# Products of key features and values in tiles of 64 columns instead of 32, in an attention and feed-forward layer

## What is computed

```python
q = heads(query, Wq, bq, Sq)            # 16 heads of 32
k = heads(key, Wk, bk, Sk)
v = heads(value, Wv, bv, Sk)
q_prime = relu(einsum('bhnd,fd->bhnf', q, Wqf))     # 64 features per head
k_prime = relu(einsum('bhnd,fd->bhnf', k, Wkf)) * mask
kv = einsum('bhnf,bhne->bhfe', k_prime, v)          # 64 x 32 per head
qkv = einsum('bhmf,bhfe->bhme', q_prime, kv)
k_sum = sum(k_prime, axis=2)
qk_sum = einsum('bhmf,bhf->bhm', q_prime, k_sum)
out = (qkv / (qk_sum + 1e-8)) @ Wo.T + bo
```

## Time and profile before

| | us |
|---|---|
| median of 3 runs | 432.66 (428.31 to 433.16) |
| the profiled execution, its own time | 431.65 |
| its span, first to last instruction | 429.6 |
| mean granted TensorE clock, share of full speed | 0.995 |
| TensorE busy (MATMUL) | 411.4 |
| weight loads busy | 284.4 |
| VectorE busy | 342.3 |
| ScalarE busy | 286.5 |
| GpSimd busy | 145.8 |

### The profile page before, as it was taken

One profiled execution on the slowest core, in us unless ns is written; L12 is line 12 of the kernel. 1 busy time (PEld: TensorE's weight loads), 2 busy tenths in 40 slices (PEclk: granted clock), 3 DMA queues, 4 the chain that ended last, 5 costly groups with the idle time before them and its releaser, 6 DMA issues.

```text
span 429.6 us, 11266 instructions
## 1 busy us (share of the span) xinstructions
PE 411.4 (96%) x4804; PEld 284.4 (66%) x4835; DVE 342.3 (80%) x505; ACT 286.5 (67%) x406; POOL 145.8 (34%) x290
## 2 busy tenths in 40 slices
PE   8989999999999999999989999999999999999995
PEld 4879899988878945844754575575567566464443
DVE  4644659658679959899986897999998798998982
ACT  5655989892155287778449747765873878939960
POOL 0000000003054722483371545547325523344660
PEclk9989999999999999999999999999999999999999
DMA  7992474632050300113323033031213021413065
GB/s 235 418 403 74 169 278 159 287 120 82 24 198 5 108 19 2 32 31 87 73 38 63 0 88 76 11 75 50 51 41 70 14 50 27 84 62 75 1 146 124
DMA packets 51170, 42.42 MB, mean 99 GB/s; under 512 B 43056, under 2 KB 44080, under 8 KB 49200
## 3 DMA queue, kind: packets, MB, share of 16 engines
q1 hardware_dynamic: 51120, 41.70, 32.9%
HBM read 27.01 MB, written 4.19 MB: 73 GB/s over the span
## 4 chain that ended last, share of the span: by engine, by line
PE 52%; DVE 21%; issue 7%; ACT 7%; POOL 6%; DMA 6%; SPq 0%; DVEq 0%; ACTq 0%
PE ps L538 11%; PE ps L407 11%; PE ps L358 6%; PE ps L360 5%; PE ps L359 5%; PE ps L555 4%; DVE zb L974 3%; PE ps L429 2%; PE ps L514 2%; DMA xqT<-xqb 2%; PE ps L448 2%; DVE rows_of L922 2%; DVE tk L985 2%; DVE qol L933 1%; DVE rows_of L917 1%
## 5 line engine op out<-in xcount | busy, mean ns | idle before, releaser
L538 PE MATMUL ps<-tg,xqT 128*128 128x512 bf16 x243 | 58.1, 380 | 4.6 <-DMA xqT<-xqb 2.9
L538 PE MATMUL ps<-tu,xqT 128*128 128x512 bf16 x245 | 59.1, 379 | 1.3 <-issue 0.6
L555 PE MATMUL ps<-td,yqT 128*128 128x512 bf16 x202 | 45.9, 379 | 1.1 <-DMA yqT<-yqb 0.7
L538 PEld LDWEIGHTS ps<-tg,xqT 128*128 128x128 bf16 x256 | 23.5, 98 | 33.1 <-DMA xqT<-xqb 4.0
L538 PEld LDWEIGHTS ps<-tu,xqT 128*128 128x128 bf16 x256 | 24.2, 98 | 31.2 <-issue 3.0
L721 ACT ACTIVATE rb<-zb 128x1024 f32<-128x1024 f32 x29 | 30.6, 1055 | 20.7 <-DVE zb L974 20.5
L974 DVE TENSOR_TENSOR zb<-ps,rb 128x1024 f32<-128x1024 f32 x29 | 35.3, 1218 | 8.2 <-ACT rb L717 8.0
L358 PE MATMUL ps<-aph,wqh 128*128 128x256 f32 x128 | 37.2, 290 | 0.0
L360 PE MATMUL ps<-aph,wkl 128*128 128x256 f32 x124 | 35.4, 286 | 1.8 <-issue 1.8
L985 DVE TENSOR_REDUCE tk<-zb 128x1 f32<-128x1024 f32 x30 | 36.2, 1207 | 1.0 <-POOL zb L1189 0.7
L358 PE MATMUL ps<-aph,wkh 128*128 128x256 f32 x124 | 36.2, 292 | 0.6 <-issue 0.6
(11 more groups left out here) (153 smaller groups left out, 1037.1 us busy)
## 6 DMA issues: line engine op xcount, KB each, us to landing
xs<-in_wg_dram SPq DMA_DIRECT2D x4, 1024.0 KB, 13.9
xs<-in_wu_dram SPq DMA_DIRECT2D x4, 1024.0 KB, 6.6
xs<-in_wd_dram SPq DMA_DIRECT2D x4, 1024.0 KB, 7.9
xs<-in_x_dram SPq DMA_DIRECT2D x8, 512.0 KB, 4.9
out_dram<-xs SPq DMA_DIRECT2D x15, 256.0 KB, 2.0
craw<-in_ctx_dram SPq DMA_DIRECT2D x7, 512.0 KB, 5.8
xs<-in_wk_dram SPq DMA_DIRECT2D x4, 256.0 KB, 5.0
xs<-in_wv_dram SPq DMA_DIRECT2D x4, 256.0 KB, 6.6
```

What stands on the lines that cost most here:

```text
L538: k = pe.matmul(ps[:, b0 + n, :], xqT[:, i % 3, kc, :], tern[w][:, o:o + 512], start=kc == 0, stop=kc == KC - 1)
L555: k = pe.matmul(ps[:, D_BANK[i], :], yqT(i)[:, j, :], tern[2][:, 512 * j:512 * j + 512], start=j == 0, stop=j == 15)
```

## The change

In `key_values`, the inner loop runs over the two heads of a pair instead of over four pieces of 32 features. Each matmul takes all 64 features of a head as its stationary operand, and the two matmuls of a pair lie side by side as two tiles of 128 rows by 64 columns. There are 32 matmuls for a sequence instead of 64, and 256 instead of 512 in all. The results lie in the same places of the same bank.

```diff
@@ -439,13 +439,12 @@
                 for half in range(2):
                     for pr in range(4 * half, 4 * half + 4):
                         for t in range(2):
-                            for c in range(4):
-                                i = 2 * b + t
-                                h = head(pr, c // 2)
-                                o = 256 * (h % 4) + 64 * (h // 4) + 32 * (c % 2)
-                                out = ps[32 * c:32 * c + 32, KV_BANK[b] + half, 33 * (pr % 4):33 * (pr % 4) + 33]
-                                left, right = kp[:, t, o:o + 32], vt[:, i % 4, h // 2, 34 * (h % 2):34 * (h % 2) + 33]
-                                k = pe.matmul(out, left, right, start=t == 0, stop=t == 1, tile_position=(0, 32 * c))
+                            for hd in range(2):
+                                i, h = 2 * b + t, head(pr, hd)
+                                o = 256 * (h % 4) + 64 * (h // 4)
+                                out = ps[64 * hd:64 * hd + 64, KV_BANK[b] + half, 33 * (pr % 4):33 * (pr % 4) + 33]
+                                left, right = kp[:, t, o:o + 64], vt[:, i % 4, h // 2, 34 * (h % 2):34 * (h % 2) + 33]
+                                k = pe.matmul(out, left, right, start=t == 0, stop=t == 1, tile_position=(0, 64 * hd))
                     k.then_inc(*key_values_done.now(b, half))
```

## The result

| | before | after |
|---|---|---|
| median of 20 runs each | 431.61 us (427.83 to 433.16) | 434.83 us (432.36 to 436.19) |
| ratio after to before | | 1.0082, 95% interval 1.0064 to 1.0100 |
| profiled execution, its span | 429.6 us | 430.5 us |

The changed kernel is slower by 0.8%, some 3.5 us by the ratio and 3.2 by the medians. In two later comparisons it was 1.0100 (1.0061 to 1.0140) and 1.0103 (1.0065 to 1.0142) times before. The forecast was 436.5 us, +1.1%. It was made for a profiled execution; that one took 432.49 us, and the two later profiled ones of the same kernel 437.35 and 432.86.

The account below looks back on a forecast made before the run. TensorE, busy 96% of the span, was taken as the bound: profiled 431.65 us plus 4.8 for seven longer blocks plus 0.1 for the eighth gave 436.5 us, range 431 to 441.

Parts of the forecast that it names:

- The load sets the turn: In a tile of 64 columns, the weight load, not the 33-column stream, sets each pass at 57 ns; chance 0.79.
- Block +0.69 us: Each changed block: last start at 1.82 us (0.11 first turn plus 30 turns of 57 ns) against 1.13 before.
- the 86 ns: Longest turn considered, from line 429's whole blocks: 1.37 us for 16 turns; would add 1.6 us a block.
- Seven blocks on the path: TensorE alone bounds the first seven blocks, so each adds its full 0.69 us: +4.8 us.
- The eighth hidden: Behind the eighth block TensorE waits 0.8 us for xqT, so only 0.1 us counted, between nothing and 0.33.
- "Issue" waits left at nothing: Two TensorE waits for no other engine, 0.8 us in all, might go or move; counted zero, kept for the range.
- All inputs come through TensorE, so the rest is rigid: Later stages were taken as a rigid chain, so delay in the blocks would not be swallowed there.
- Both rules of the Trainium skill: MATMUL starts never closer than about 25 ns; loads overlap a MATMUL only across row groups. The prediction set rows against both.
- Handed out: Rival: instruction hand-out, 8.9 ns a pass, paces the block; 0.56 us less each, total about 427.5 us; chance 0.07.
- One after the other: Rival: load and stream cannot overlap within a tile; turn 82 ns, +1.41 us a block, total 442.1 us; chance 0.08.
- No change: Rival: something else is late where the blocks end, so the time stays at 431.65 us; chance 0.06.

Follow-up runs that it names:

- e2: The changed kernel, its two tiles each loading only the first 32 of a head's 64 columns (half the products left out): 428.62 us, ratio 0.9956.
- e3: The changed kernel, tiles of 64 columns, each matmul streaming 1 column instead of 33: 441.08 us, ratio 1.0253.
- e4: The kernel before, four tiles of 32 columns, each matmul streaming 1 column instead of 33: 430.21 us, ratio 1.0010.
- e7: The kernel before with tiles of 64 columns in the first seven blocks and 32 in the eighth: 432.85 us, ratio 1.0054.
- e11: The kernel before, its eighth block alone with 32 matmuls loading 32 columns each (half that block's products left out): 428.42 us, ratio 0.9947.
- e12: The kernel before with tiles of 64 columns in the seventh block alone: 430.24 us, ratio 0.9976 to before.
- e5: The changed kernel again, unchanged, for a second profile: 436.09 us.
- e10: The changed kernel again, unchanged, for a third profile and more runs: 435.83 us.
- e1: The kernel before once more, unchanged, for a second profile: 431.16 us, ratio 1.0008.
- e8: The kernel before with tiles of 64 columns in the eighth block alone, run a second time: 428.56 us, ratio 0.9948.
- e9: The kernel before with tiles of 64 columns in the sixth and eighth blocks: 431.30 us, ratio 1.0024.

## Why the prediction was right

By its own steps:

- *The load sets the turn.* Right, and shown from both sides: a load of 32 columns on the same two tiles gives 1.01 us (e2), a stream of one column changes nothing (e3). The forecast turn was 57 ns, the measured one 58.5 (1.84 us less the first turn of 0.08, over 30). The time for a load of 32 columns was not right: 27 ns was worked out from 128 columns, and e2 and e4 show turns of 32 to 34. The forecast did not use it.
- *Block +0.69 us.* Measured +0.71 from first start to last, +0.73 to the follower. Two small parts were off and cancelled, which is luck: the first turn is 0.08 us, while 0.11 was line 429's (0.03 too long once), and the turn is 58.5 and not 57 (0.045 too short over 30). On the long side, the 86 ns were divided by 16 where 16 passes have 15 intervals; it is 91 ns, and changes nothing in the forecast. The records are longer than forecast, a MATMUL's 223 ns and not 200, a load's 138 and not 130.
- *Seven blocks on the path.* Right: the value products behind a block begin 0.73 later each time.
- *The eighth hidden.* Right. 0.1 was forecast; the stage from it to the gate product is 0.1 shorter than before, the wait of 0.8 for xqT being gone, and 0.1 to 0.3 longer than in e7, e11 and e12 with their narrow eighth block.
- *"Issue" waits left at nothing.* This is the term of the sum that was mis-sized. Between 30 and 130 us they are gone in all six profiles with 256 or 288 of these matmuls (after, e2, e3, e5, e7, e10), and each of the eight with 448 or more has at least one (in e11 the one at 35 alone). Over the first six blocks the change gives +2.7 to +3.5 and not 6 x 0.73 = 4.4: 0.9 to 1.7 us come back. Before has 0.9 us of such stalls and e1 1.5. The 0.8 that the prediction kept for its range was read from one profile, where the wait in the sixth block stands as 0.2 and makes the block 0.37 longer.
- *All inputs come through TensorE, so the rest is rigid.* Not quite. Behind the seventh block 0.7 us are the block, and up to 2.6 more came (0.7 to 1.0 of VectorE beside GpSimd, 1.6 of half clock), in some executions. Neither is bound to the wide seventh block: the first is in e8 and e9, the second in e9. Whether the change makes them more frequent is open.
- *Both rules of the Trainium skill* that were set against rows fell. TensorE: Matmul & The Clock Gate, section "Wait — 56ns, not 53.3ns?", has no two starts closer than 25 ns; 128 passes over four tiles run at 8.7 ns each on average (e4). The Trainium skill, the same page, section "Part 3: Packing small matmuls — row/col tiling", lets a load overlap a stream only in another row group; here both use all 128 rows, and the turn is the same 58 ns with 33 streamed columns and with one. The measurement decides in both.
- *Rivals.* Handed out: refuted for after by e2, which has as many passes and ends sooner; in before a limit common to the four tiles costs some 0.1 us of a block (e4, and before, against e2). One after the other: refuted by e3. No change: refuted by the ratio.

Net: +5.1 for seven blocks, -0.9 to -1.7 for the stalls, and the rest in both directions, +3.5 to +4.4 by the ratios against +4.9 forecast. The range held it. A part of the difference between the three ratios can be told from the runs' granted clocks. At full clock after took 433.10 us (7 runs of the first comparison), 433.18 (one, e5) and 433.34 (two, e10); before took 429.84 (7 runs beside e5) and 430.05 (9 beside e10). That is +3.3. The ratios of e5 and e10 are larger by their runs below full clock, nine of twelve, which lie 2.5 to 4.3 us above the others, where those of before lie 0.7 to 2.9 above theirs. These are few runs, and why they lose more is open.

## What to carry to other kernels

In this kernel a tile of 64 columns has a new pass every 58 ns whether 33 columns are streamed or one, and a tile of 32 columns every 32 to 34 ns. So half as many matmuls on half as many tiles was no gain: compare passes per tile times the time of a load. Splitting the stationary operand over four tiles instead of two was faster although it doubled the instructions, 1.13 us a block against 1.84. Whether this holds for other types and for longer streams was not tried. And before a change of 0.5% is credited to its mechanism, run a kernel that has the same program length and not the mechanism (e11 here).

## What was not expected of the hardware

- Kernels that differ in TensorE's program alone differ in the issue times of DMA transposes on another engine's queue 50 to 280 us later (1.34 against 2.35 to 2.82 us; for the last pair 3.0 to 3.7 against 2.6). Those with the longer first and the shorter last issue came out some 0.5% faster than their wide blocks account for. The cause is open, and that the 0.5% comes through these times is not shown.
- The granted clock fell to half for 3.4 us behind blocks of wide loads with one streamed column (e3), with TensorE recorded busy throughout; behind the same blocks with 33 columns it did not. A busy record does not by itself keep the clock.
- Idle waits of 1.8 us near 21 us and of 2 us and more before the last down product are in some executions followed by such a stretch and in others not. It costs 1.6 to 1.7 us each time. The runs' mean granted clocks say that this makes most of the spread between runs of one kernel: of the 29 runs of before beside e1, 12 at full clock have a median of 429.5 us, 10 at a mean of 0.995 or 0.996 have 430.9, and 7 at 0.991 or 0.992 have 432.9. One stretch of 3.4 us at half clock lowers the mean of 430 us by 0.004.
